# The FFN's 1168 output columns in three pieces of 384, 384 and 400 instead of 512, 512 and 144, with new orders on the engines

## The reference, cut to what matters

```python
def _hydra(u, ...):                       # applied twice
    zxbcdt = u @ in_w.T                   # z, xBC, dt
    xBC = silu(_causal_conv(xBC, conv_w, conv_b))          # 7 taps
    y = shifted forward scan + shifted backward scan + xs * (xs @ fcD_w.T + D)
    yz = y * silu(z)
    return (yz * rsqrt(mean(yz**2) + 1e-5) * norm_w) @ out_w.T

h = concat([cls_tok, s4d_tokens(x)])
h = h + attn(layernorm(h))     # attn: x + up(mixed(gelu(x @ w_down.T), hydra(hydra(..))))
h = h + ffn(layernorm(h))
# ffn
base_out = x @ base_W.T + base_b                           # 1024 columns
probs = softmax(x @ router_W.T + router_b)                 # 15 columns
w = weights of the 8 experts from the top 8 probs
hh = x @ A.T                                               # 8 experts x rank 16 = 128 columns
lora = ((hh * w) @ B) * 2.0
return base_out + lora
```

## Time and profile before

| | |
|---|---|
| median of 3 runs | 2296.11 us (2288.2 to 2297.39) |
| the profiled execution | 2292.67 us |
| its span, first to last instruction | 2290.9 us, mean granted TensorE clock 0.981 |
| busy share of the span | TensorE 92%, its weight loads 77%, VectorE 77%, ScalarE 66%, GpSimd 46% |
| costliest line | L1396, the FFN's matmuls: 3 x 1560, 602.3, 554.0 and 552.7 us busy |

### The profile page before, as it was taken

How to read it: one execution, slowest core, us unless ns; L and a number is a source line. 1 busy time by engine, 2 the same in 40 slices (tenths; PEclk the granted TensorE clock), 3 DMA queues, 4 the chain that set the end, 5 groups by cost and what they waited for, 6 DMA issues and landing times.

```text
span 2290.9 us, 50769 instructions
## 1 busy us (share of the span) xinstructions
PE 2118.5 (92%) x13871; PEld 1773.2 (77%) x13871; DVE 1768.5 (77%) x4943; ACT 1516.3 (66%) x2844; POOL 1057.3 (46%) x1291
## 2 busy tenths in 40 slices
PE   0266999999999999999999999999999999999998
PEld 0144888888888888888888888888888888887876
DVE  7455788887888878888788777888778888787774
ACT  4365767667676676766767667676676766766552
POOL 6664454444544445444454444544445444453331
PEclk9966999999999999999999999999999999999999
DMA  5201121222212222112221222211222112221211
GB/s 171 63 15 39 59 68 38 63 67 67 66 37 64 67 67 67 38 62 67 67 66 37 63 67 67 67 38 62 67 67 67 37 63 67 67 67 31 70 40 34
DMA packets 79029, 136.91 MB, mean 60 GB/s; under 512 B 10560, under 2 KB 52288, under 8 KB 78976
## 3 DMA queue, kind: packets, MB, share of 16 engines
q1 hardware_dynamic: 77536, 130.45, 18.7%
q10 hardware_dynamic: 1440, 5.83, 0.7%
HBM read 59.51 MB, written 76.74 MB: 59 GB/s over the span
## 4 chain that ended last, share of the span: by engine, by line
PE 52%; issue 22%; POOL 8%; DVE 8%; ACT 5%; POOLq 1%; DVEq 0%; ACTq 0%
PE bank L1396 21%; POOL CB L784 5%; PE bank L1502 3%; PE bank L1492 3%; PE bank L1457 3%; PE bank L1552 3%; PE bank L1468 2%; PE bank L1580 2%; PE bank L1599 2%; POOL XD L728 1%; DVE W L1090 1%; PE bank L1510 1%; PE bank L1568 1%; PE bank L1528 1%; PE bank L1558 1%
## 5 line engine op out<-in xcount | busy, mean ns | idle before, releaser
L1396 PE MATMUL bank<-w_hi,XHI 128*128 128x512 f32 (+1 forms) x1560 | 602.3, 386 | 1.4 <-DVE XLO L1279 1.4
L1396 PE MATMUL bank<-w_hi,XLO 128*128 128x512 f32 (+1 forms) x1560 | 554.0, 355 | 0.0
L1396 PE MATMUL bank<-w_lo,XHI 128*128 128x512 f32 (+1 forms) x1560 | 552.7, 354 | 0.0
L1031 DVE SCALAR_TENSOR_TENSOR CX<-bank,cw,CX 128x252 f32<-128x252 f32 (+5 forms) x804 | 352.7, 462 | 66.3 <-ACT CX L827 66.1
L1396 PEld LDWEIGHTS bank<-w_hi,XLO 128*128 128x128 f32 x1560 | 295.2, 189 | 46.3
L1396 PEld LDWEIGHTS bank<-w_lo,XHI 128*128 128x128 f32 x1560 | 295.7, 190 | 44.4
L1396 PEld LDWEIGHTS bank<-w_hi,XHI 128*128 128x128 f32 x1560 | 295.6, 189 | 41.0 <-DVE XLO L1279 1.6
L812 ACT ACTIVATE T<-bank 64x512 f32<-64x512 f32 x256 | 151.4, 592 | 254.3 <-PE bank L1492 249.6
L784 POOL TENSOR_TENSOR CB<-CB,CM 48x252 f32<-48x252 f32 (+5 forms) x402 | 263.1, 654 | 72.6 <-ACT CM L812 24.4
L741 POOL TENSOR_TENSOR RS<-VE,half_neg 128x1 f32<-128x1 f32 x65 | 35.5, 546 | 480.7 <-DVE VE L1223 480.7
L1492 PE MATMUL bank<-VB,W 128*128 128x256 f32 x512 | 143.9, 405 | 91.4 <-DVE W L1096 89.4
(11 more groups left out here) (257 smaller groups left out, 5189.7 us busy)
## 6 DMA issues: line engine op xcount, KB each, us to landing
carried<-T SPq DMA_DIRECT2D x65, 512.0 KB, 4.5
T<-carried SPq DMA_DIRECT2D x65, 512.0 KB, 3.8
out<-HB SPq DMA_DIRECT2D x129, 256.0 KB, 3.1
XTC<-in_x SPq DMA_DIRECT2D x64, 128.0 KB, 3.5
w_raw<-in_w_all ACTq DMA_DIRECT2D x8, 584.0 KB, 11.4
tables<-tab SPq DMA_DIRECT2D x8, 560.0 KB, 3.9
TB<-tables SPq DMA_DIRECT2D x64, 70.0 KB, 2.8
carried<-U SPq DMA_DIRECT2D x65, 64.0 KB, 3.5
```

Of the source, the lines that this page charges most:

```text
L1031: inc(STT(CX[:, c, :, s:CS], src[:, :, 0:CS - s], cw[:, c, k:k + 1], CX[:, c, :, s:CS], ALU.mult, ALU.add), "conv")
L1396: ins = mm(bank[:, 0:c1 - c0], xs_[:, 1 - p, k, :], ws[:, k, c0:c1], start=(c0 == HID and k == 0 and n == 0), stop=(last == k and n == 2))
```

## The change

The 1168 columns are cut at 384 and 768. The first two pieces (384 columns each) go to bO[0] and bO[1], the third (256 columns of the base output, then hh, then the router, 400 together) to bR, whose group now begins with `start=True` on its first matmul and then gets the bias of its 256 base columns. So `bases` works on pieces 0 and 1 and `route` on piece 2. The third piece's lora product doesn't add to its base columns: it is a group of its own in columns 256 to 511 of bR, after `turn_h`, and VectorE adds the two parts to HB one after the other (`final_first`, and `final(0)`). `lora(n)` and `final(n)` go in the order LORA = (2, 0, 1). `turn_h` waits for `final_first` (fin=1), the store for four finals, and the counts of o go from 2 to 3.

The lists of the four compute engines are new; on TensorE decay_sums stands between grams and turn_xs. Waits with o=2 become o=3.

```diff
+    PIECES = ((0, 384), (384, 768), (768, 1024))
+    LA, LR = 256, 384
...
-        bO = banks[0:2]
+        bO = banks[0:3]
         bR = banks[2]
+        LORA = (2, 0, 1)
...
-                    def final(h):
+                    def final(n):
                         if E:
-                            wait(dve, te, o=h + 1)
-                            c = slice(HALF * h, HALF * (h + 1))
-                            inc(TT(HB[:, 1 - p, c], bO[h][:, :], HB[:, 1 - p, c], ALU.add), "fin")
+                            wait(dve, te, o=n + 1)
+                            c0, c1 = PIECES[LORA[n]]
+                            part = bR[:, LA:512] if LORA[n] == 2 else bO[LORA[n]][:, 0:c1 - c0]
+                            inc(TT(HB[:, 1 - p, c0:c1], part, HB[:, 1 - p, c0:c1], ALU.add), "fin")
+
+                    def final_first():
+
+                        if E:
+                            wait(dve, te, rt=1)
+                            c0, c1 = PIECES[2]
+                            inc(TT(HB[:, 1 - p, c0:c1], bR[:, 0:LA], HB[:, 1 - p, c0:c1], ALU.add), "fin")
 
...
-                    def ffn(c0, c1, bank, ks, last=None):
+                    def ffn(c0, c1, bank, ks, start, last=None):
 
                         for k in ks:
                             for n, (xs_, ws) in enumerate(((XHI, w_hi), (XHI, w_lo), (XLO, w_hi))):
                                 ins = mm(bank[:, 0:c1 - c0], xs_[:, 1 - p, k, :], ws[:, k, c0:c1],
-                                         start=(c0 == HID and k == 0 and n == 0), stop=(last == k and n == 2))
+                                         start=(start and k == 0 and n == 0), stop=(last == k and n == 2))
+                                if start and k == 0 and n == 0:
+                                    mm(bank[:, 0:LA], row_sel[:, :], base_bias[:, c0:c0 + LA], start=False, stop=False)
                         return ins
 
                     def route(a, b):
@@ -1403,33 +1418,35 @@
                                 if isinstance(i, int) and te == 0:
                                     pe.wait_ge(w_rest, len(RAW))
                                 wait(pe, te, xlo=2)
-                                wait(pe, te - 1, hwl=1)
-                            ins = ffn(HID, FW, bR, range(a, b), last=KC - 1)
+                                wait(pe, te - 1, fin=LORA.index(2) + 2)
+                            ins = ffn(PIECES[2][0], FW, bR, range(a, b), True, last=KC - 1)
                             if b == KC:
                                 inc(ins, "rt")
 
                     def bases(h, a, b):
                         if E:
+                            c0, c1 = PIECES[h]
                             if a == 0:
                                 if isinstance(i, int) and te == 0:
                                     pe.wait_ge(w_rest, len(RAW))
                                 wait(pe, te, xlo=2)
-                                wait(pe, te - 1, fin=h + 1)
-                                mm(bO[h][:, :], row_sel[:, :], base_bias[:, HALF * h:HALF * (h + 1)], start=True, stop=False)
-                            ffn(HALF * h, HALF * (h + 1), bO[h], range(a, b))
+                                wait(pe, te - 1, fin=LORA.index(h) + 2)
+                                mm(bO[h][:, 0:c1 - c0], row_sel[:, :], base_bias[:, c0:c1], start=True, stop=False)
+                            ffn(c0, c1, bO[h], range(a, b), False)
 
                     def turn_h():
                         if E:
-                            wait(pe, te, hw=1)
+                            wait(pe, te, hw=1, fin=1)
                             inc(tr(bR[:, 256:256 + P], HW[:, :], ident[:, :]), "trh")
 
-                    def lora(h):
+                    def lora(n):
                         if E:
                             wait(pe, te, hwl=1)
-                            c = slice(HALF * h, HALF * (h + 1))
-                            mm(bO[h][:, :], HWS[:, 0, :], lb_hi[:, c], start=False, stop=False)
-                            mm(bO[h][:, :], HWS[:, 1, :], lb_hi[:, c], start=False, stop=False)
-                            inc(mm(bO[h][:, :], HWS[:, 0, :], lb_lo[:, c], start=False, stop=True), "o")
+                            c0, c1 = PIECES[LORA[n]]
+                            bank = bR[:, LA:512] if LORA[n] == 2 else bO[LORA[n]][:, 0:c1 - c0]
+                            mm(bank, HWS[:, 0, :], lb_hi[:, c0:c1], start=(LORA[n] == 2), stop=False)
+                            mm(bank, HWS[:, 1, :], lb_hi[:, c0:c1], start=False, stop=False)
+                            inc(mm(bank, HWS[:, 0, :], lb_lo[:, c0:c1], start=False, stop=True), "o")
 
```

## The result

The changed kernel takes 2269.93 us (median of five runs, 2267.07 to 2274.9), the kernel before on the same chip 2293.52: ratio 0.9894, 95% interval 0.9878 to 0.9909. It is 1.1% faster, in the direction that I forecast and inside the range, but with 24 us instead of 49. The profiled execution has a span of 2266.9 us.

The account below looks back on a forecast made before the run. TensorE's issue of its list was taken as the bound, 31.80 us an iteration; -1.09 + 0.16 - 0.17 + 0.25 + 0.1 = -0.75, times 65 iterations is 49 us off 2292.7: 2244 us, range 2212 to 2282.

Parts of the forecast that it names:

- pieces, no waits: FFN matmuls on TensorE: 384, 384 and 400 columns cost less than 512, 512 and 144, saving 1.09 us an iteration.
- the lists' own (seams, turn_d): TensorE order: two more 512-column matmuls following transposes cost +0.16 us, turn_d(0) no longer starting late gives -0.17.
- new waits: TensorE waiting at project_bc for layer_out's copy, +0.25 us, and at turn_h and lora(0) for VectorE, together +0.1.
- rival C: VectorE's stretch from gated_b to weighted_lo is the path and its waits eat the gain: 2260 to 2300, chance 0.15.
- rival D: Slower, about 2315: VectorE's stretch over 0.75 us longer than walked, softplus and decays_forth(0) lengthened by GpSimd's adds; chance 0.05.
- the 8.66: VectorE's time in us without idling from gated_b to weighted_lo in the old trace, the base for estimating final_first's end.
- slack of 0.4 us at residual(1): On VectorE, residual(1) waits for up(1) in the forecast's walk; this 0.4 us spoke against a slower result.
- a floor that the narrow piece pays: FFN matmuls on TensorE: 0.111 us under each that doesn't shrink with columns, paid by the 144-column piece on 24 an iteration.
- turn_a(1) not held back by the early table load: ScalarE's silu_z with its 1.28 us table load, moved ahead of keep_turned(0), was costed at nothing.
- Rival E: Matmul cost is a straight line through 144 and 512 columns, so the pieces save nothing: 2315, chance 0.03.

Follow-up runs that it names:

- both moves: Changed kernel with final_first moved behind router(0) and bases(0, 3, 4) moved ahead of project_bc: 2199.99 us, 0.9582 of before.
- new lists with old pieces: Changed kernel's lists with the old pieces of 512, 512 and 144 columns, and bases(0, 3, 4) ahead of project_bc: 2256.02 us, 0.9842 of before.

## Why the prediction was wrong in size

Per iteration, with the forecast beside what the runs give:

| term | forecast | measured | from |
|---|---|---|---|
| pieces, no waits | -1.09 | -0.88 | both moves against new lists with old pieces |
| the lists' own (seams, turn_d) | -0.01 | -0.57 | new lists with old pieces and cover, against before |
| new waits | +0.35 | +1.13 | the change against both moves |
| sum | -0.75 | -0.32 | 31.485 - 31.80 |

The step that failed is the one called new waits. It named the right steps (project_bc behind layer_out, turn_h behind final_first), but its sizes were not right, and rival C, the waits that eat the gain, is what happened: 2260 to 2300 with a chance of 0.15.

- turn_h, for which I took 0.1, is where the path runs. In the window shown project_out starts at S = 1037.88 and final_first ends at S + 10.44, where I had S + 9.45 to S + 10.05: gated_b came 0.07 later, and VectorE's stretch was 9.32 (9.19 in the other kind of iteration) and not 8.4 to 9.0. TensorE was there at S + 9.97 (forecast 9.6 to 9.7).
- project_bc: the copy was done at S + 1.67 (1039.55), 0.04 later than forecast, but project_bc started 0.24 after that in one kind of iteration and 0.10 in the other, and not at once: 0.52 and 0.38 of waiting instead of 0.25. My 0.03 to 0.04 for a hand-off didn't hold here. My sum took the two waits as independent. Both are in the period, but where the first goes and the stretch stays, the second grows by as much. What the first wait does beyond that is to make up(0) and up(1) later, and with them VectorE's residual steps.
- That, and the holding of VectorE's steps by GpSimd's adds, is what the walk lacked. I took VectorE's durations from the trace before and named the adds as a risk (rival D) without a price of their own. That trace has held steps in it (softplus(4), 16 elements, takes 0.69 at 1025.63, beside an add), so the 8.66 was no fixed sum of steps: which of them are held depends on when they come. The slack of 0.4 us at residual(1), which was to take this up, wasn't there: in the window shown it starts at 1045.55, and up(1) is through at 1045.13.

The two moves add up: 0.34 for final_first, 0.78 for the base (31.485 - 30.70), 1.13 for both. The 0.34 is final_first's own length, taken out of the path. The 0.78 is the shorter stretch. Of it the holding is about 0.44 (31.485 - 31.04, the period with shortened adds; 28 us), and most of the rest is VectorE's waiting at the residual steps.

That the change came out faster at all is in part luck. By the table, pieces and new waits alone make +0.25 an iteration; the lists' own -0.57, which I had at nothing, made it a gain.

What held: the distances of 384 and 400 columns, a floor that the narrow piece pays, turn_a(1) not held back by the early table load, and that TensorE without waits is the bound (2200). Rival E, the straight line, is out: at 384 columns it asks 0.190.

The lists' own -0.57 I had at nothing (-0.17 at turn_d(0), +0.16 for two more seams). Means over the steady loop show where it is. The start of turn_d(0), late before, brings 0.19, about as forecast. From the start of down() to the next grams() it takes 2.59 before and 2.24 with the new lists, which is 0.35 more; all other steps, seams among them, make up 0.03 together. Of it, 0.21 is that turn_d(1) started late before:

```profile
1031.63 1.95 PE L1502 MATMUL bank<-XHT,wdT 128*128 128x128 f32 x16
1033.58 0.66 PE L1457 MATMUL bank<-ident,T 128*128 128x128 f32 x4
```

The 1.95 are 1.79 with the new lists. The list before has ScalarE's silu_x with its table load ahead of split_hi(0), which split_lo(0) and then turn_d(1) wait for; the new one has split_hi(0) first. I had costed the moves on ScalarE at nothing. No run moves them alone, so this cause is read from the rows and not shown.

## What to carry to other kernels

When an engine that never waited gets less work, price the gain at what the other engines can deliver: walk the chain that it waits for, and move out of that chain whatever has its data early (final_first could stand 9 us sooner at no cost). Try the order before shortening anything: one matmul group moved by one place was worth twice the whole change, and not by the wait that it covered, but because it let VectorE's steps start earlier and fall between GpSimd's adds. A floor per matmul belongs to its neighbours as much as to itself: read it in the sequence in which it will stand.

## What the runs showed of the hardware

A 16-element step of VectorE from SBUF to SBUF takes 0.16 to 0.18 us, but 0.61 or 0.65 when it starts early in one of GpSimd's adds, and then ends 0.03 us after that add (1043.99 against 1043.96; 918.20 against 918.17). This holds for a tensor_scalar (mean 387 ns) and for a scalar_tensor_tensor (380) alike, and goes when the adds are cut to one column (169 and 167). It doesn't hold for every small step: the 16-element reciprocal of softplus(3) takes 0.24 us in the changed kernel whether it starts in an add (54 times) or not (13 times). A step that arrives in the gap between two adds isn't held (0.16 at 1026.79). The Trainium skill (SBUF — State Buffer, section SBUF: two separate sides) has the rule: a VectorE step in a two-port mode, or one with two SBUF inputs beside a GpSimd step that reads SBUF, and the GpSimd step take the shared ports as an exclusive lock for a whole instruction. The trace agrees for the steps with two SBUF inputs, with those numbers; which mode the tensor_scalar runs in, no run shows. The price here: 0.45 us lost by a step that was 0.15 us late.
